# A graph layer, an LSTM cell and a slice attention on one core: another order for the start, and GpSimd's gathers paced by TensorE

## What is computed

```
n    = layernorm(x)
agg  = segment_sum(n[src], dst)                     # 6250 x 256
h    = relu(agg @ W_rel + n @ W_root)               # 6250 x 512
gates i, g, o = h @ W_ih.T                          # three gates of 512
x    = x + (sigmoid(o) * tanh(sigmoid(i) * tanh(g))) @ W_fc
m    = layernorm(x)
w    = softmax((m @ W_x @ W_slice) / temp)          # 8 heads x 64 slices
tok  = (w.T @ (m @ W_fx)) / sum(w)                  # attention among the 64 tokens of a head
x    = x + (w @ attention(tok)) @ W_out
```

## Time and profile before

| | |
|---|---|
| median of three executions | 1899.89 us |
| the three | 1910.17, 1899.89, 1882.88 us |
| span of the profiled execution, first to last instruction | 1305.9 us |
| TensorE busy in the span | 1195.5 us (92%) |
| GpSimd busy in the span | 841.4 us (64%), 851 gathers |
| first gather | 69.7 us |
| end of turn 0's work on TensorE, turn 1 begins | 120.5 us |
| last turns over, end part begins | about 1206 us |

### The profile page before, as it was taken

How to read it: one execution, slowest core, us unless ns; L and a number is a source line. 1 busy time by engine, 2 the same in 40 slices (tenths; PEclk the granted TensorE clock), 3 DMA queues, 4 the chain that set the end, 5 groups by cost and what they waited for, 6 DMA issues and landing times.

```text
span 1305.9 us, 25399 instructions
## 1 busy us (share of the span) xinstructions
PE 1195.5 (92%) x8519; PEld 1062.2 (81%) x8519; DVE 814.4 (62%) x2352; ACT 609.5 (47%) x1225; POOL 841.4 (64%) x883
## 2 busy tenths in 40 slices
PE   1066998999999999999999999999999999999998
PEld 0064887988888888888888888888988888898798
DVE  5662455675667656766666566756675667546665
ACT  4721335454544455444535454545444554455432
POOL 3467777777777777777777777777777777700000
PEclk9986999999999999999999999999999999999999
DMA  7764345445544454445444554455444544423399
GB/s 237 258 211 119 111 125 146 137 115 146 145 137 127 131 145 135 135 122 145 144 129 121 144 145 135 115 145 146 136 119 138 145 136 132 127 67 95 109 333 288
DMA packets 127895, 191.81 MB, mean 147 GB/s; under 512 B 55661, under 2 KB 88403, under 8 KB 127819
## 3 DMA queue, kind: packets, MB, share of 16 engines
q0 software_dynamic: 41008, 111.77, 29.6%
q1 hardware_dynamic: 74852, 57.47, 15.5%
q10 hardware_dynamic: 11979, 21.94, 5.0%
HBM read 159.02 MB, written 32.92 MB: 147 GB/s over the span
## 4 chain that ended last, share of the span: by engine, by line
POOL 45%; PE 28%; issue 16%; ACT 3%; DVE 3%; DMA 3%; SPq 1%; POOLq 0%; DVEq 0%; ACTq 0%
POOL ring L658 45%; PE ps L344 6%; PE ps L346 6%; PE ps L345 6%; PE ps L1019 3%; PE ps L1120 2%; DMA ring<-in_x 1%; DMA table<-ring 1%; ACT ps L782 1%; ACT L764 1%; PE ps L1108 1%; ACT x L772 1%; PE ps L965 1%; ACT ring L721 1%; DVE oneh L1454 0%
## 5 line engine op out<-in xcount | busy, mean ns | idle before, releaser
L658 POOL DMA_INDIRECT ring<-table,sidx x851 | 812.8, 955 | 268.8 <-issue 268.5
L344 PE MATMUL ps<-h_h,wih_h 128*128 128x256 f32 x1200 | 346.2, 289 | 0.0
L345 PE MATMUL ps<-h_l,wih_h 128*128 128x256 f32 x1200 | 339.6, 283 | 0.0
L346 PE MATMUL ps<-h_h,wih_l 128*128 128x256 f32 x1200 | 339.4, 283 | 0.0
L1019 PE MATMUL ps<-ring,oneh 128*125 128x512 f16 x974 | 231.3, 383 | 14.3 <-DMA ring<-table,sidx 14.2
L344 PEld LDWEIGHTS ps<-h_h,wih_h 128*128 128x128 f32 x1200 | 229.7, 191 | 3.5 <-issue 0.4
L345 PEld LDWEIGHTS ps<-h_l,wih_h 128*128 128x128 f32 x1200 | 229.9, 192 | 1.7
L346 PEld LDWEIGHTS ps<-h_h,wih_l 128*128 128x128 f32 x1200 | 229.7, 191 | 0.0
L797 ACT ACTIVATE gate<-ps,bgate 128x256 f32<-128x256 f32 x300 | 125.5, 471 | 205.4 <-PE ps L346 204.4
L1019 PEld LDWEIGHTS ps<-ring,oneh 128*125 128x125 f16 x974 | 132.0, 138 | 82.6 <-DMA ring<-table,sidx 21.7
L1454 DVE TENSOR_SCALAR oneh<-iota,rel 128x125 f16<-128x125 f16 x974 | 166.5, 285 | 1.8
(11 more groups left out here) (227 smaller groups left out, 2504.9 us busy)
## 6 DMA issues: line engine op xcount, KB each, us to landing
ring<-table,sidx POOLq DMA_INDIRECT x851, 2.8
swt_d<-swt ACTq DMA_DIRECT2D x25, 500.0 KB
gate<-swt_d SPq DMA_DIRECT2D x19, 500.0 KB, 5.8
table<-ring SPq DMA_DIRECT2D x11, 512.0 KB, 7.0
xn<-table SPq DMA_DIRECT2D x25, 224.0 KB
xin<-in_x SPq DMA_DIRECT2D x25, 224.0 KB
res<-xin SPq DMA_DIRECT2D x25, 224.0 KB
ring<-in_x SPq DMA_DIRECT2D x9, 512.0 KB, 6.9
```

The costliest lines, as they stand in the source:

```text
L344: eng.matmul(dst, wh, xh, start=first, stop=False)
L345: eng.matmul(dst, wh, xl, start=False, stop=False)
L346: return eng.matmul(dst, wl, xh, start=False, stop=last)
L658: pool.indirect_dma_start(ring[:, j, :], None, table, bass.IndirectOffsetOnAxis(ap=sidx[:, odd * SLOTS + j:odd * SLOTS + j + 1], axis=0)). ...
```

## The change

It has two parts.

**The start.** The twelve chunks of `x` get rooms of their own (`x_room`, in the place where `wih_h` and `wih_l` are written later), so that all loads of `x` are issued at once; the freed place in `ring` gives six `lt` tiles for three (`TILES`). `dst` goes straight into SBUF, without the copy in HBM; the two copies of `src` and `dst` to HBM are issued after all stores of `table`, and pair 0's lists come from the inputs. The eight bias vectors are loaded as rows (4 partitions of 512 bytes each, `brow`), are turned by one transposition on TensorE (into `bvec`), and stand with the other small loads behind stores 5 to 9. `W_rel` and `W_root` come behind stores 3 and 4, `W_x` behind store 5. On VectorE `plan_a` and `plan_c` are cut in pieces that stand between chunks, and `plan_f` stands ahead of the last two `ln_low`. ScalarE loads its table for the square root by a dummy instruction at the start. TensorE transposes `W_x` only after the small loads. The semaphores of the last part are used for the chunks too, so their counts there start higher (`F_IN0`, `F_RES0`, `F_ST0`).

**The pace.** Ahead of ten of a pair's twelve groups of gathers GpSimd also waits for a stage of TensorE (`pace`).

```diff
+    TILES = 6
+        with nc.sbuf_tensor("x_room", [P, 2 * KT * MT * P], F32) as x_room:
+            pass
+        brel = bvec[:, 0, :]
+        brow = agg[0:8 * KT, 0, 0:P]
-        lx = [scratch[:, k * words:(k + 1) * words].rearrange("p (r c) -> p r c", c=C) for k in range(3)]
+        lx = [x_room[:, k * words:(k + 1) * words].rearrange("p (r c) -> p r c", c=C) for k in range(NCH)]
...
-                if k >= 4:
-                    wait_rows(sp, k - 4)
...
+            for k in range(4):
+                load_chunk(k)
+            rows = a["dst"].rearrange("(p b) -> p b", b=ER)
+            sp.dma_start(edge_i[0:WN, 0:ER], rows).then_inc(ld_tab, 16)
...
+            for k in range(4, NCH + 1):
+                load_chunk(k)
...
+            for k in range(NCH - 1):
+                store_chunk(sp, k)
+                if k in (1, 2):
+                    if k == 1:
+                        sp.wait_ge(ld_edges, 16 * 3)
+                    load_edges(0, 0, k - 1, idx_in[k - 1], a["src"], a["dst"])
...
+                if 5 <= k <= 8:
+                    bias(2 * k - 10, 2 * k - 8)
...
+            for q in range(TILES):
+                sp.wait_ge(ln_out[q], 16 * len(range(q, NCH + 1, TILES)))
+            sp.dma_start(srcp[0:E].rearrange("(a b) -> a b", b=ER), a["src"].rearrange("(a b) -> a b", b=ER)).then_inc(ld_edges, 16)
+            sp.dma_start(dstp[0:E].rearrange("(a b) -> a b", b=ER), a["dst"].rearrange("(a b) -> a b", b=ER)).then_inc(ld_edges, 16)
+            sp.wait_ge(ld_edges, 16 * 5)
...
+            def pace(p, n):
+
+                stage, done = {
+                    1: (gate_mm, MT // 2 * (p - 2) + 2), 2: (lg_mm, 2 * (p - 2)), 3: (gate_mm, MT // 2 * (p - 2) + 3),
+                    4: (gate_mm, MT // 2 * (p - 2) + 4), 5: (gate_mm, MT // 2 * (p - 2) + 5),
+                    7: (swt_mm, 2 * (p - 2)), 8: (xt_done, p), 9: (y_mm, p - 1), 10: (h_mm, 2 * p),
+                    11: (x2t_mm, p - 1)}.get(n, (None, 0))
+                if stage is not None:
+                    after(pool, stage, done)
...
                         for q in range(3):
+                            pace(p, 6 * e + 3 * k + q)
...
+            act.activation(mx8[:, 0:1], eps[:, :], ACT.Sqrt)
...
+            pe.wait_ge(ld_small, 16 * NSMALL)
+            pe.transpose(ps[:, HB, 0:8 * KT], brow, ident[0:8 * KT, 0:8 * KT])
             pe.wait_ge(ld_wx, 16)
...
+            plan_f(rooms)
             ln_low(dve, NCH - 1)
             ln_low(dve, NCH)
-            plan_f(rooms)
             bias_rows()
```

More of the change, by code:

```diff
@@ L232, in build_program @@
         ld_rows = sem("ld_rows")
-        ln_in = [sem(f"ln_in{k}") for k in range(4)]
-        ln_out = [sem(f"ln_out{k}") for k in range(3)]
+        f_in = [sem(f"f_in{k}") for k in range(FB)]
+        f_res = [sem(f"f_res{k}") for k in range(FB)]
+        f_st = [sem(f"f_st{k}") for k in range(FB)]
+        ln_in = [sem(f"ln_in{k}") for k in range(4)] + f_in + f_res
+        ln_out = [sem(f"ln_out{k}") for k in range(3)] + f_st[0:TILES - 3]
+        assert len(ln_in) == NCH and len(ln_out) == TILES and NCH == 2 * TILES
+        F_IN0, F_RES0, F_ST0 = 16, [16] * (FB - 1) + [32], [32 if k < TILES - 3 else 0 for k in range(FB)]
         consts, dve_step, pe_step, pool_step = (
@@ L395, in _, with bias @@
                              didx[:, 0:n]).then_inc(ld_edges, 16)
[L396 to L402, removed]
-            r4 = raw[:, 0:4 * HID].rearrange("p (k n) -> p k n", n=HID)
[L405 to L410, removed]
-                loads.append((bxc, a["b_x"].rearrange("(k p) -> p k", p=P)))
-                with nc.allow_non_contiguous_dma(reason="bias vectors go down the partitions once"):
-                    for to, v in loads[first:end]:
-                        sp.dma_start(to, v).then_inc(ld_small, 16)
+            for k in range(4, NCH + 1):
+                load_chunk(k)
+            r4 = raw[:, 0:4 * HID].rearrange("p (k n) -> p k n", n=HID)
+            def bias(first, end):
+                loads = [a["b_rel"]]
+                for g in GATES:
+                    for b in ("b_ih", "b_hh"):
+                        loads.append(a[b][g * HID:(g + 1) * HID])
+                loads.append(a["b_x"])
+                for n, v in list(enumerate(loads))[first:end]:
+                    sp.dma_start(brow[n * KT:(n + 1) * KT, :], v.rearrange("(k p) -> k p", p=P)).then_inc(ld_small, 16)
             def load_list(to, t, base, n, done):
@@ L734, in _ @@
             act.activation(w1_h[:, :, :], raw[:, 0:4 * HID].rearrange("p (k n) -> p k n", n=HID), ACT.Copy).then_inc(w1_free, 1)
-            for q in range(3):
-                act.wait_ge(ln_out[q], 16 * len(range(q, NCH + 1, 3)))
+            for q in range(TILES):
+                act.wait_ge(ln_out[q], 16 * len(range(q, NCH + 1, TILES)))
             load_wih(act, 0, ld_wih)
@@ L889, in f_high @@
             def f_high(n, k):
[L890 removed]
+                act.wait_ge(f_in[k], F_IN0 + 16 * n + 16)
                 act.wait_ge(f_mm[k], n + 1)
@@ L1730, in f_add @@
                 dve.wait_ge(f_mm[k], n + 2)
-                dve.wait_ge(f_res[k], 32 * n + 32)
-                after(dve, f_st[k], 32 * n)
+                dve.wait_ge(f_res[k], F_RES0[k] + 32 * n + 32)
+                if not (isinstance(n, int) and n == 0):
+                    dve.wait_ge(f_st[k], F_ST0[k] + 32 * n)
                 dve.tensor_tensor(fo[k][0:WN], ps[0:WN, f_bank[k], :].rearrange("p (e c) -> p e c", e=2),
```

127 lines of the change are left out of this document (56 added, 71 removed).

## The result

| | kernel before | kernel after |
|---|---|---|
| median | 1905.03 us (4 executions, 1882.88 to 1913.32) | 1615.76 us (4 executions, 1613.92 to 1621.61) |
| ratio | | 0.854, 95% interval 0.850 to 0.859 |
| profiled execution: its own time, its span | span 1305.9 | 1621.61, span 1619.7 |

The change made the kernel 15% faster where 0.6% was forecast. The span of the kernel after is 1.9 us shorter than the execution's own time, so nearly nothing lies outside the span, and the 594 us that the prediction left there were inside. The trace of the kernel before in the earlier trace rows is of an execution in which the kernel took about 1306 us, and not of one like those timed. By their times the table's are of the slower kind.

The account below looks back on a forecast made before the run. TensorE and GpSimd were taken as both nearly full in turns of about 42.7 us, so only the beginning could gain: 11 us from an earlier first gather, 0 for the pace, 1899.9 - 11 = 1889 us, range 1850 to 1912.

Parts of the forecast that it names:

- the median of the runs is 594 us above the span; I leave that as it is: Sum: 594 us between profiled span and timed median kept unchanged, so 1899.9 - 11 = 1889 us.
- Late it is not: Pace: stages the ten waits need are done 18 to 20.3 us before GpSimd asks, so no wait binds.
- the 594 us lie inside the turns: Rival: timed executions are longer everywhere or TensorE slower, pace binds; 1871 us, or 1848 and beyond; chance 0.16.
- the 13 us of idle time: Same rival: all TensorE idle time in the turns goes, 0.4 x 23 turns x 1.455 = 13 us gained.
- The pace costs nothing: Ten GpSimd waits between gathers: hidden in the 0.30 us gaps and never late, cost 0.
- slower rival: Waits not hidden between gathers, 3 us more a turn, 66 us in all: 1955 us; chance 0.06.
- The beginning: Before turn 0: first gather at about 59 instead of 69.74, 11 us earlier, passed on to the whole span.
- little gain: Rival: DMA engines stay at 0.76 in the beginning or stores flush late; gain 4, 1896 us; chance 0.16.
- The term of 4 us, a stall of ScalarE for tile 6: Beginning: chunk 6 wants its tile at about 26, store 0 lands about 30; 4 us lost.
- The order that it rests on: SyncE's queue: store 0 waits behind all queued loads of x and dst, which take until 27 us.
- The last full high half: ScalarE in the beginning: without stall it would end at 44.5 instead of 60.7 us.
- VectorE is faster too: Beginning: per chunk, GpSimd (2.12 us) and VectorE are faster than ScalarE (2.90 or 3.38 us), so ScalarE sets the pace.

Follow-up runs that it names:

- waits alone: Kernel before with the ten waits of GpSimd for TensorE's stages, old beginning kept: 1604.16 us (0.838) on chip 3, 1310.57 us (1.000) on chip 6.
- prompt chip: Chip (1, 6, 14) on which TensorE's signals are not late; the unchanged kernel before takes 1307 to 1311 us.
- the six sets: Follow-up executions, each set on one chip with the kernel before beside it: chips 3, 14, 6, 1, 0, 1; kernel before 1903 to 1924 or 1307 to 1311 us.
- late chips: Chips (0 and 3) on which TensorE's signals come late; the unchanged kernel before takes 1902.75 and 1923.71 us.
- twelve waits: Kernel before with waits for TensorE ahead of all twelve groups: 1307.88 us (1.000) on chip 14, 1311.79 on chip 6; not run on chips 0 or 3.

## Why the prediction was wrong

**The step that failed** is "the median of the runs is 594 us above the span; I leave that as it is". It took the difference for something outside the kernel's work, and with it every stretch, wait and gap of the recorded execution for those of the timed ones. In an execution as timed (chip 3) the turns are 56 to 79 us long, GpSimd is idle 852 us and not 269, and ScalarE waits 363 us for signals that no row of before shows.

The pricing of the pace fell with it. "Late it is not" took its margin of about 18 to 20 us from the 42.7 us turns of that trace. In the kernel after as timed, GpSimd's gathers sit idle 172.3 us for signals marked remote, and 47.9 us for gate, graph and transposition stages of TensorE that only the new waits name. Waits that were put at nothing because they never bind do bind there, and by the run with the waits alone (0.838) the gain comes with them.

**The rival "the 594 us lie inside the turns"** named the right place and the right sign: "GpSimd runs ahead to the limit of its slots, does nine gathers in a row and stops, and the pace would bind and spread them". Gathers 513.43 to 523.49 are nine in a row. Its size was wrong by a factor of ten (29 us against 289), because it gave the pace only the 13 us of idle time of the recorded turns; the timed ones had 11 to 28 us of idle time in all turns from the second to the last but one. A rival that says "the trace is not of such an execution" can't be priced from that trace; its bound was the 594 us themselves, and the range should have gone there. The sentence in it on the Trainium skill, "Runtime: NRT & Kernel Launch" (about 15 us around a kernel), was the better guide. An execution's own time and its span differ by 1.9 us here, and either number says that 594 us are no overhead. The rival's chance of 0.16 was too small for that.

**The pace costs nothing**: right on a prompt chip, waits alone 1.000 (0.999 to 1.001), gaps of 0.30 us, turns of 42.6 to 42.9 us in all but three of 24. The stages are done well ahead of their waits there, as reckoned. The slower rival is refuted by the same row.

**The beginning**: right in sign, half in size. Forecast 11 us, measured 5.4 to 5.7 in the first gather and 6.2 us (1311.09 - 1304.85) in the time, near the rival "little gain" (4 us), but for another reason. Densely loaded it was: 369 GB/s from 15 to 27 us where 285 was assumed. The term of 4 us, a stall of ScalarE for tile 6, did not come. The order that it rests on held: store 0, issued at 13.7 us, had landed at 26.2, behind the last load of `x` at 24.9, as assumed and as the rule cited with that term has it. But 26.2 is earlier than the 30 reckoned, and ScalarE was ready to write chunk 6 only at 30.8. The last full high half was at 48.5 by the sum, at 54.4 measured (53.40 + 1.04); from there 9.9 us to the gather, where 10.55 was reckoned. What was put at nothing in the sum is ScalarE's waiting for VectorE: 2.34, 2.85, 2.34 and 2.62 us ahead of four chunks. Two smaller terms were off as well: its first row began at 8.57 us and not at 7.3, and its rows overlap, so that a chunk of three rows takes 2.6 us and not 2.90. The kernel after on chip 6, ScalarE, VectorE, GpSimd:

```profile
37.26 2.07 ACT L738 ACTIVATE ring<-x_room,nmr,rstd 128x256 f32<-128x256 f32 x4 [2.85 <-DVE nmr L1345]
```
```profile
33.68 0.14 DVE L1344 RECIPROCAL rstd<-sd 128x4 f32<-128x4 f32 x1
33.86 3.37 DVE L1345 SCALAR_TENSOR_TENSOR nmr<-mv,rstd 128x4 f32<-128x4 f32 x1
```
```profile
32.99 4.20 POOL L619 TENSOR_TENSOR ring<-ring 128x1024 f16<-128x1024 f32 x2
```

A step that takes 0.16 us elsewhere in this trace, on four numbers a partition, takes 3.37 us and ends when GpSimd's two low halves end (37.19). Ahead of each of the four waits a VectorE instruction of 1.9 to 3.4 us ends with a low half of GpSimd. Over the beginning this step takes 628 ns at the mean against 253 before. The prediction's "VectorE is faster too" counted the work of each engine by itself. The Trainium skill, "SBUF — State Buffer", section "Who interferes with whom", says that the port pair that the two engines share is an exclusive lock, and that a VectorE instruction with two SBUF inputs contends with a GpSimd instruction that reads SBUF. The trace agrees (3.37 us, to the end of GpSimd's row). That the chunks meet this more often because they now run closer together is likely, but was not tried.

**What stays open.** Why TensorE's signals are late on some chips. The ends of matmuls are modelled, so whether the semaphore's rise or the matmul's completion is late can't be told from these rows. A rival that no run excludes is the recording itself. Every execution of the six sets has a span, so all were recorded, and on late chips many rises are missing from the trace: 13,395 in all for the kernel before on chip 3 against 26,201 in the earlier trace rows's trace, 201 against 295 of the 300 of ScalarE's gates, 3,068 against 13,505 of the gathers' landings (16 each). Whether the kernel before takes 1900 us on such a chip when nothing is recorded is not known. Whether bytes or number of gathers decide. Whether twelve waits, or stops for landings, do better than ten on a late chip.

## What to carry to other kernels

When the span of a recorded execution and the median differ by more than some microseconds, the trace may not be of what was timed: before anything is priced from it, read a second trace of the same kernel, on the chip of the times. If there is none, the range of the forecast has to reach as far as the difference. A wait marked "remote" or "unknown queue" in a program of one core is a question about the semaphore: look up who raises it, and compare with the end of that engine's last row. Here a wait for a stage that is done long before was free (1.000), and it bounded the damage where signals come late (0.838). A wait that always stops, for one's own landings, cost its full length (1.282).

## What the runs showed of the hardware

- The same program takes 1903 to 1924 us at the median on chips 0 and 3 and 1307 to 1311 us on chips 1, 6 and 14, each within 2% of itself but for one execution of 1384.3 us on chip 14.
- On the first kind TensorE's signals arrive late, by 8.2 us at the mean and up to 23.8 (chip 3), once indirect gathers of 128 rows of 1 KB have followed each other every 1.25 us for over 4 us; with one gather of three left the kernel takes 1324 us (chip 0). No recorded signal of ScalarE, VectorE or GpSimd is late there. ScalarE and VectorE do their work in nearly unchanged time (614.6 and 815.1 us busy against 609.5 and 814.4).
- The lower clock comes with TensorE's idle time: the mean granted clock is 0.844 for the kernel before on chip 3. With levels of 1.2 and 2.4 GHz that is 2 x 0.156 x 1914.1 = 597 us at the lower one, against 259 us for the kernel after (0.92) and 31 us for it on chip 6 (0.988). TensorE's busy time is 144 of the 608 us longer, and that is all that the lower clock can explain directly.
- On late chips the trace lacks many rises of semaphores: 13,395 recorded for the kernel before on chip 3, 26,201 in the execution of 1305.9 us.
